# First batch's state-space scan placed in the second batch's attention, second expert layer in two parts

## The reference

```python
x = L0_attn_x                                             # 2 x 1024 x 128
xn = _layernorm(x, axis=-1)
x = x + _L0_attn_ref(xn, ...) + _L0_ffn_ref(xn, ...)      # 8 heads; 14 experts, top 1
xn = _layernorm(x, axis=-1)
x = x + _L1_attn_ref(xn, ...) + _L1_ffn_ref(xn, ...)      # scan; 8 experts, top 2

# _L1_attn_ref, d_inner = 256, 16 states
u, res = x @ W_in, halves;  u = silu(u)
delta = softplus(u @ W_delta + b_delta)
Bm, Cm = u @ W_B, u @ W_C
def step(h, inp):
    d_t, B_t, C_t, u_t = inp
    dA = jnp.exp(d_t[..., None] * A)
    h = dA * h + d_t[..., None] * B_t[:, None, :] * u_t[..., None]
    y_t = jnp.einsum('bdn,bn->bd', h, C_t)
    return (h, y_t)
y = (scan of step + u * D_param) * silu(res)
out = y @ W_out
```

## Time and profile before

| | before |
|---|---|
| median of 3 runs | 881.31 us |
| lowest and highest run | 878.81 and 1666.01 us |
| profiled execution | 883.31 us, its span 881.5 us |
| PE busy, weight loads busy | 680.0 us (77%), 474.4 us |
| DVE busy | 546.7 us (62%) |
| ACT busy | 415.1 us (47%) |
| POOL busy | 300.3 us (34%) |
| PE in the 40 slices | eight or nine tenths busy in both attentions and the first experts, mostly six or seven tenths in the last twelve slices |

### The profile page before, as it was taken

One profiled execution on the slowest core, in us unless ns is written; L12 is line 12 of the kernel. 1 busy time (PEld: TensorE's weight loads), 2 busy tenths in 40 slices (PEclk: granted clock), 3 DMA queues, 4 the chain that ended last, 5 costly groups with the idle time before them and its releaser, 6 DMA issues. The chain is left out here.

```text
span 881.5 us, 11690 instructions
## 1 busy us (share of the span) xinstructions
PE 680.0 (77%) x3456; PEld 474.4 (54%) x3468; DVE 546.7 (62%) x820; ACT 415.1 (47%) x824; POOL 300.3 (34%) x211
## 2 busy tenths in 40 slices
PE   4889999999989689999999898501766666675764
PEld 2656666666659566666666654100555555561222
DVE  5264333343323234433445448977999998999998
ACT  1255555555525355455555668422454552553330
POOL 0012122101100022112211100786776763768882
PEclk9589999999979999999999998855699997996998
DMA  9200000000556500000000000113254552440112
GB/s 306 60 3 10 10 9 12 6 3 7 152 156 214 164 10 10 10 9 9 6 3 7 6 1 1 45 39 119 65 153 147 177 156 83 157 142 24 36 33 57
DMA packets 45761, 57.63 MB, mean 65 GB/s; under 512 B 6049, under 2 KB 32418, under 8 KB 45730
## 3 DMA queue, kind: packets, MB, share of 16 engines
q1 hardware_dynamic: 32994, 46.23, 16.8%
q0 software_dynamic: 3072, 6.30, 2.4%
q10 hardware_dynamic: 9664, 4.72, 1.8%
HBM read 43.60 MB, written 13.63 MB: 65 GB/s over the span
## 5 line engine op out<-in xcount | busy, mean ns | idle before, releaser
L437 POOL TENSOR_TENSOR QL<-QF,QH 128x512 fp32r<-128x512 f32 x32 | 40.6, 1268 | 409.4 <-ACT QH L558 409.4
L1353 DVE TENSOR_REDUCE nmax<-PS 128x1 f32<-128x128 f32 (+7 forms) x128 | 96.6, 756 | 116.2 <-PE PS L828 114.7
L566 ACT COPY PT<-PS 128x512 f32<-128x512 f32 (+1 forms) x192 | 85.8, 482 | 139.0 <-PE PS L840 138.9
L856 PE MATMUL PS<-PT,V 128*128 128x512 f32 (+3 forms) x384 | 151.0, 505 | 0.2 <-ACT PT L566 0.2
L482 POOL TENSOR_TENSOR YA<-YA,HC 128x1024 f32<-128x1024 f32 x44 | 103.9, 2362 | 53.9 <-DVE HS L1514 53.3
L815 PE MATMUL PS<-KH,QH 128*128 128x512 f32 (+1 forms) x192 | 87.3, 455 | 19.6 <-POOL QL L437 19.0
L573 ACT ACTIVATE PR<-PS,nmax 128x128 f32<-128x128 f32 (+7 forms) x128 | 96.4, 753 | 5.5 <-DVE nmax L1353 5.5
L840 PE MATMUL PS<-CST,PR 128*128 128x128 f32 x576 | 85.7, 276 | 14.5 <-ACT PR L573 14.4
L840 PEld LDWEIGHTS PS<-CST,PR 128*128 128x128 f32 x576 | 68.4, 142 | 48.7 <-issue 32.1
L1047 PE MATMUL PS<-R,pickb 128*128 128x512 bf16 x58 | 23.0, 482 | 79.8 <-DVE HS L1514 34.7
L1369 DVE SCALAR_TENSOR_TENSOR X<-PS,rinv,X 128x128 f32<-128x128 f32 x128 | 36.1, 345 | 74.1 <-PE PS L878 74.1
(11 more groups left out here) (200 smaller groups left out, 1287.0 us busy)
## 6 DMA issues: line engine op xcount, KB each, us to landing
mw<-in_w SPq DMA_DIRECT2D x40, 512.0 KB, 4.4
mw<-in_w SPq DMA_DIRECT2D x16, 321.0 KB, 4.1
more_w<-in_w SPq DMA_DIRECT2D x16, 321.0 KB, 3.6
rows_in<-zero SPq DMA_DIRECT2D x18, 256.0 KB, 3.5
MX<-rows_in SPq DMA_DIRECT2D x20, 128.0 KB, 4.2
rows_out<-MY ACTq DMA_DIRECT2D x20, 128.0 KB, 2.8
rows_out<-MY ACTq DMA_DIRECT2D x8, 256.0 KB, 4.3
X<-in_x SPq DMA_DIRECT2D x4, 256.0 KB, 4.2
```

The source lines that it names most:

```text
L566: nc.scalar.copy(dst, src).then_inc(s_ed, 1)
L856: r = mm(PS[:, 6, lo:BANK], V[:, b * TB + j, :], PT[b][:, 4 * group + j, lo:BANK], start=j == 0, stop=True, skip_group_check=True)
L1353: nc.vector.tensor_reduce(nmax[:, i % 4:i % 4 + 1], sc[:, 0:(i + 1) * P], AX_X, ALU.max, negate=True).then_inc(s_nm, 1)
```

## The change

The second layer of the first batch starts as soon as the first expert layer has stored its rows. POOL gathers that batch's eight tiles, and `combine_first`, the statistics, `rows_out`, the transposes, `inner`, `step_sizes` and the rows B and C of the first batch come ahead of `attention(1)`. Head 8 carries that batch's routing (24 tiles for it alone) and the four DVE steps of its softplus. Each of heads 9 to 15 carries two states of the first batch: DVE does two drives, two scans and two products for each between its steps of the head, ACT two decays. In these states the rows B[n] and C[n] are not spread by PE; the 32 rows are copied to SBUF, stored in DRAM (`bc_rows`), and SP loads each one broadcast over the partitions into BS and CS, two buffers each. So all inputs of DVE's instructions of these states lie in SBUF (the tensor ROOM, in which nearly all working tensors of both phases now lie). The running y is no longer added by POOL's arithmetic: POOL issues a DMA that adds HC to YA0 in SBUF. States 14 and 15 of the first batch follow behind the attention.

Behind the attention come the second batch's gathers, projections, routing (another 24 tiles) and softplus, then its 16 states as before, with B and C spread by PE. The second expert layer now has 48 tiles in 24 pairs. The second matrices of all eight experts are loaded once (`second_w`), and only the first matrices (256 KB each) are loaded for each tile; PE and SP both read each tile's expert number with `value_load`. Four pairs are done ahead of the second batch's scan, two beside each of its states 0 to 9, and none beside states 10 to 15. The 32 gathers of the results go six to a state in these. The skip term u * D is computed by ACT into the y that is then added to. Keys, values and turned probabilities have one buffer each instead of one for each batch.

The core of the diff follows, engine by engine.

The tables: expert layer 2 becomes two layers of 24 tiles or 12 pairs each, one for each batch.

```diff
-MOE = [(14, 1, 2), (8, 2, 4)]
...
+MOE = [(14, 1, 2), (8, 2, 4), (8, 2, 4)]
+ROWS = [(0, NT), (0, TB), (TB, NT)]
...
+TILES = [4 * -(-(((t1 - t0) * P * k + e * (P - 1)) // P) // 4) for (e, k, _), (t0, t1) in zip(MOE, ROWS)]
 QUADS = TILES[0] // 4
 PAIRS = TILES[1] // 2
-LATE = PAIRS - (STATE - 4)
-EARLY = 4
+AHEAD = 4
+LATE = (2 * PAIRS - AHEAD) // 2
```

```diff
+            def attention_loads_second():
+
+                def spread_b_row(n):
+                    if n >= 2:
+                        sp.wait_ge(s_xsn, 2 * n - 2)
+                    sp.dma_start(BS[:, n % 2, :], bcd[n:n + 1, :].broadcast_to([P, T])).then_inc(s_xbl[n % 2], 16)
+
+                def spread_c_row(n):
+                    if n >= 2:
+                        sp.wait_ge(s_xhc, 2 * n - 2)
+                    sp.dma_start(CS[:, n % 2, :], bcd[STATE + n:STATE + n + 1, :].broadcast_to([P, T])).then_inc(s_xcl[n % 2], 16)
...
+                load_wq(HEADS, 0, 0, 2 * HEADS - 2)
+                load_wq(HEADS + 1, 1, 1, 2 * HEADS)
+                sp.wait_ge(s_bcc, 1)
+                sp.dma_start(bcd[:, :], DU0[0:32, 0, :]).then_inc(s_bcd, 16)
+                sp.wait_ge(s_bcd, 16)
+                spread_c_row(0)
+                spread_c_row(1)
+                load_wq(HEADS + 2, 2, 0, 2 * HEADS + 2)
+                sp.wait_ge(s_du, 1)
+                sp.wait_ge(s_yi, 2)
+                spread_b_row(0)
+                spread_b_row(1)
+                for h in range(1, HEADS):
+                    spread_b_row(2 * h)
+                    if h + 2 < HEADS:
+                        load_wq(HEADS + h + 2, h + 2, h % 2, 2 * (HEADS + h) + 2)
+                    spread_c_row(2 * h)
+                    spread_b_row(2 * h + 1)
+                    spread_c_row(2 * h + 1)
...
+            def second_expert_loads():
+                sp.wait_ge(s_we, 4 * HEADS)
+                for e in range(MOE[1][0]):
+                    sp.dma_start(second_w[:, e, :], A["w_1"][e][:, 4 * P:8 * P]).then_inc(s_mw2, 16)
...
+                    for i in range(2):
+                        e = sp.value_load(eid[1][0:1, bass.ds(2 * p + i, 1)], min_val=0, max_val=MOE[1][0] - 1)
+                        sp.dma_start(mw1[:, 2 * s + i, :], A["w_1"][bass.ds(e, 1)].rearrange("o p n -> (o p) n")[:, 0:4 * P]
+                                     ).then_inc(s_mw1[s], 16)
```

```diff
+            def y_add(n, c):
+
+                pool.wait_ge(s_xhc, 2 * n + c + 1)
+                if n:
+                    pool.wait_ge(s_xy[c], 16 * n)
+                else:
+                    pool.wait_ge(s_yi, c + 1)
+                nc.gpsimd.dma_start(YA0[:, c, :], HC[:, c, :], accum_op=ALU.add).then_inc(s_xy[c], 16)
+
+            def attention_second():
+                query_low(HEADS, 0)
+                for t in range(TB, NT):
+                    if t == TB + 3:
+                        query_low(HEADS, 1)
+                    gather(0, 0, t, GA[:, t, :], s_g0[1])
+                query_low(HEADS + 1, 0)
+                for h in range(1, HEADS):
+                    n = 2 * h - 2
+                    y_add(n, 0)
+                    query_low(HEADS + h, 1)
+                    if h == 1:
+                        pool.wait_ge(s_slot, 2)
+                    scatter(1, range(TB * (h - 1) // (HEADS - 1), TB * h // (HEADS - 1)))
+                    y_add(n, 1)
+                    if h < HEADS - 1:
+                        query_low(HEADS + h + 1, 0)
+                    y_add(n + 1, 0)
+                    y_add(n + 1, 1)
+                for n in (STATE - 2, STATE - 1):
...
+            for t in range(TB):
+                gather(0, 0, t, GA[:, t, :], s_g0[0])
+            attention_second()
```

```diff
+                    head(g, True, g < 15, after={0: (n, 1), 2: (n + 1, 0), 3: (n + 1, 1), 6: (n + 2, 0)})
+                out_evac(0, 31)
+                keep_turned(15, 7)
+                first_decay(STATE - 2, 1)
+                out_evac(1, 32)
...
+            first_decay(STATE - 1, 0)
+            first_decay(STATE - 1, 1)
+            skip(1)
             step_sizes(1)
-            decay(0, 1, True)
...
             pair_in(0)
             pair_hidden(0)
-            beside(0, EARLY + 1, 1, 1, None)
-            decay(0, EARLY + 2, True)
-            copy_c(0, EARLY + 2)
+            pair_in(1)
+            pair_out(1, 0, None)
+            pair_hidden(1)
...
+            def beside(n, p, times):
+                pair_out(p, 1, times)
+                pair_in(p)
+                pair_hidden(p)
+                pair_in(p + 1)
+                pair_out(p + 1, 0, times + 16)
+                pair_hidden(p + 1)
...
+            with act.Fori(SHARED + 1, LATE) as n:
+                decay(n, True)
+                copy_c(n)
+                beside(n, AHEAD + 2 * n, 8 * AHEAD - 16 + 16 * n)
```

```diff
+            inner(0)
+            step_sizes(0)
+            bc_rows(0)
             attention(1)
...
+            def two_pairs(p, times, between=None):
+                first, second = experts_of(p), experts_of(p + 1)
+                turn_pair(p, 0, times)
+                hidden_pair(p, 0, times)
+                turn_pair(p + 1, 1, times)
+                result_pair(p, first)
+                hidden_pair(p + 1, 1, times)
+                if between:
+                    between()
+                result_pair(p + 1, second)
...
+            two_pairs(0, 1)
+            two_pairs(2, 2)
+            scan_out(0)
             pe.wait_ge(s_r3, 1)
             pe.wait_ge(s_as, 2)
...
+            spread_b(0, False)
...
+            with pe.Fori(SHARED + 1, LATE) as n:
+                spread_c(n)
+                two_pairs(AHEAD + 2 * n, n + AHEAD // 2 + 1, lambda: spread_b(n + 1))
+            spread_c(LATE)
```

```diff
+            def first_drive(n, c):
+
+                if c == 0:
+                    dve.wait_ge(s_xbl[n % 2], 16 * (n // 2 + 1))
+                    if n:
+                        dve.wait_ge(s_xsn, 2 * n - 1)
+                drive = BS[:, n % 2, :] if c else DB
+                tt(drive, DU0[:, c, :], BS[:, n % 2, :], ALU.mult).then_inc(s_xdb, 1)
+
+            def first_scan(n, c):
+
+                dve.wait_ge(s_xdA, 2 * n + c + 1)
+                dve.wait_ge(s_xdb, 2 * n + c + 1)
+                if n or c:
+                    dve.wait_ge(s_xhc, 2 * n + c)
+                drive = BS[:, n % 2, :] if c else DB
+                nc.vector.tensor_tensor_scan(HS0, DA[:, c, :], drive, 0.0, ALU.mult, ALU.add).then_inc(s_xsn, 1)
+
+            def first_c(n, c):
+
+                dve.wait_ge(s_xcl[n % 2], 16 * (n // 2 + 1))
+                dve.wait_ge(s_xsn, 2 * n + c + 1)
+                if n:
+                    dve.wait_ge(s_xy[c], 16 * n)
+                tt(HC[:, c, :], HS0, CS[:, n % 2, :], ALU.mult).then_inc(s_xhc, 1)
+
+            def first_state(n):
...
+                for g in range(9, 16):
+                    n = 2 * (g - 9)
+                    head(g, True, g < 15, g > 9, after={
+                        0: (lambda: first_drive(n, 0), lambda: first_drive(n, 1)),
+                        1: (lambda: first_scan(n, 0), lambda: first_c(n, 0)),
+                        2: (lambda: first_scan(n, 1),),
+                        3: (lambda: first_c(n, 1), lambda: first_drive(n + 1, 0)),
+                        4: (lambda: first_drive(n + 1, 1),),
+                        5: (lambda: first_scan(n + 1, 0),),
+                        6: (lambda: first_c(n + 1, 0),),
+                        7: (lambda: first_scan(n + 1, 1), lambda: first_c(n + 1, 1))})
...
+            combine_first(0)
+            statistics(2)
+            variance(2)
+            rows_out(2)
+            dve.wait_ge(s_as, 1)
+            link(ts(a_sc[:], a_sc[:], -1.0, None, ALU.mult))
+            bc_copy()
+            attention_second()
...
+            first_state(STATE - 2)
+            route(2)
+            first_state(STATE - 1)
+            take_ranks(2)
+            place(2)
+            for part in step_parts(1):
+                part()
             gated(0)
...
+            pick_weights(2)
+            bc_parts()
+            scan_out(0)
```

955 lines of the change are left out of this document (481 added, 474 removed).

## The result

The changed kernel takes 920.95 us, the median of 4 runs from 918.41 to 924.14, against 882.2 us for the kernel before (the median with a fourth run). The ratio is 1.0455, with an interval from 1.0402 to 1.0507. It is slower by 4.6%, where no change was forecast, and the time lies outside the range of 848 to 910. Its profiled execution has a span of 922.3 us, against 881.5.

What follows compares the result with a forecast made beforehand. PE was taken to bound the second attention and DVE the part behind it; 881.5 + 49.5 + 9.0 + 45.5 - 7.4 - 98.3 = 879.8, forecast 880 us, no change that can be told, range 848 to 910 for 8 in 10.

Steps and rivals of the forecast that it cites:

- 5b: Second batch's ten states with two expert pairs each: chain through ACT and PE's loads make 12.0 us each, 117.1 in all.
- 5a: End of the attention to the first pairs of the second batch's state 0: logarithm behind two pairs, 70.2 us.
- term 3: Heads 9 to 15 with two states each: DVE becomes the bound, 31.5 us a head, +45.5 us.
- Term 1: New stretch between the experts and head 8, first batch's gathers, projections and step sizes: +49.5 us, bounds 44 and 54.
- Term 2: Head 8, with the first batch's routing and step-size parts on DVE: 27.8 us instead of 18.8, +9.0.
- Term 4: End of the attention: loses transposes and inner projections, last scan and product lie beside PE's output parts, -7.4 us.
- Rival A: Second batch's ten states: the pairs fit under DVE's state, sum 848 us, or 856 at half way; chance 0.18.
- Step 5c: Six late states without pairs: six gathers in each of the first five make POOL the limit, 65.7 us.
- The tail: Behind the last HC, at the kernel's end: 15.6 us, unchanged.
- C: Heads with states: accumulating y DMAs land late and DVE waits, 899 us, or 919 at 13 us each; chance 0.18.
- D: Heads with states: POOL's DMA issues keep DVE out as its products do, 40 us more, 920; chance 0.04.
- The slower side: Whole kernel: chance 0.22 of a time over 899 us, made of C and D.

## Why the prediction was wrong

The forecast was 879.8 us for the span, and 922.3 came. Three steps failed most. In 5b PE's loads of expert numbers were given 1.4 us of a state (0.9, and 0.5 for the clock) and cost 3.0. In 5a a stall beside the scatters, 12 us, was missing. In term 3 ACT's selector copy (3.6 us in head 10) and PE's lower clock in the heads were costed nowhere. That the states lie beside the heads at about the forecast price was right. Point by point, by its own steps:

- **Term 1, the stretch ahead of head 8: +49.5 forecast, +54.6 measured.** The experts' last store was issued 3.1 us later than before, and the eight inner projections took 9.1 us and not 7, their first 4.3 us at the lower clock. A size, just above its bound of 54; over the profiles of the variants this point stood 46.1 to 54.6 us later than in the kernel before, and the forecast lies among them.
- **Term 2, head 8: 27.8 forecast, 26.5 measured.**
- **Term 3, heads 9 to 15: +45.5 forecast, +52.6 measured** (227.6 us for seven). The head was right at 31.24 for 31.5 (the works listed sum to 27.9 and not 28.2; DVE was busy for 28.5). The step that was missing is ACT's selector copy: the prediction costed it nowhere, and it held head 10 up by 3.6 us. Heads 9 and 12 were long too (34.8 and 33.0). In both PE's clock was at its lower level for some 6 us behind its wait of 2.59 us for POOL's query step (0.53 from 402 to 409 us, 0.54 from 501.4 to 508), and DVE then waited 2.2 and 2.1 us for a score; in head 11 the same stretch had 0.69 and the wait was 1.2. The prediction took PE's part of a head at the clock of before. This was read from the traces and no run tests it, and it leaves some 2 us of head 9 open.
- **Term 4: -7.4 forecast, -1.1 measured.** The sixteen matmuls of the last head's product with V took 7.9 us instead of 5.8, their first 4.3 us at the lower clock. The three inner projections that were taken out had mostly lain beside DVE's turn, so taking them out brought 1.2 and not 2.7. And the last scan and product ended at 615.8 us, ahead of those sixteen matmuls (616.0) and not beside them, so that the 3.9 subtracted for them was not there in full.
- **Step 5a, E to the first drive: 70.2 forecast, 84.6 measured.** The mechanism (logarithm behind the pairs, loads behind state 15) was right, and without the stall 72.6 and 72.9 came. The stall of 12 us beside an unbroken row of scatters was not foreseen, and no row of the kernel before showed it: its own row of scatters had no pairs beside it.
- **Step 5b, the ten states: 117.1 forecast, 129.8 measured,** from the first drive (713.0) to that of state 10 (842.8). The chain without the loads was right, 10.6 forecast and 10.7 measured. The term that was mis-sized is the loads: they were given 0.9 us and their clock 0.5, and cost 3.0 in all in the loop, since they left PE without work for 2.5 us and the pair behind them ran at the lower clock. The seven states of the loop took 13.6 for 12.0. State 0 took 12.9 for 8.4, and 8.9 with the loads away; states 1 and 2 took 10.8 in the mean. Rival A did not hold in the changed kernel; its state came only with the loads moved and ACT's order changed, at 9.5 us between its 8.5 and 10.2.
- **Step 5c, the six late states: 65.7 forecast, 63.8 measured.** This step was right: 17.5 us to the end of the first quarter for 17.7, then a quarter each 10.1 us in the mean for 11.0 (8.7, 10.4, 12.6 and 8.7, with none, one, two and no issue stretched), and 6.0 behind for 4.0.
- **The tail: 15.7, as forecast.**

The first four terms are +17.2 off, 5a +14.4, 5b +12.7, 5c -1.9 and the tail +0.1, which makes the 42.5 between 879.8 and 922.3.

Rivals C and D fell. The accumulating transfers landed 5.7 us after their issue by the page's part on DMA issues, and no product waited for one:

```profile
ROOM<-ROOM POOLq DMA_DIRECT2D x32, 512.0 KB, 5.7
```

The estimate of 9 us had charged reading and writing in full one after the other. The rule of the Trainium skill, "SBUF — State Buffer", section "SBUF: two separate sides", that a DVE instruction with two inputs in SBUF and a GpSimd one that reads SBUF block each other fully, held in the direction that counted: the scan that began 0.08 us after the query step took its 2.28 and 1.05 more.

Five of the eight terms came out above their size and none came out far below, and no rival was made of terms that add up on one side. The slower side had only 0.22, and C and D, for which it was given, had no part in it.
